# Moving the next pair's projections, turns and Gram matrix to earlier steps of a polynomial-attention loop, and one expert's weight load behind the row scatter

## What is computed

```python
xn = layernorm(x)
# graph convolution: normalised adjacency counts times xn @ W
# attention with a polynomial in place of the exponential, 12 heads of 64:
q, k, v = (qkv[0] * SCALE, qkv[1], qkv[2])
A = einsum('bhnd,bhmd->bhnm', q, k)
numerator = 1.0 + A + 0.5 * A * A
attn = numerator / numerator.sum(axis=-1, keepdims=True)
out = einsum('bhnm,bhmd->bhnd', attn, v)      # then @ w_proj + b_proj
x = x + gnn + attention
# switch feed-forward: 8 experts, at most 195 tokens each, the best first
h = gelu(einsum('ecd,edf->ecf', buf[:E], w1) + b1)
o = einsum('ecf,efd->ecd', h, w2) + b2
x = x + where(keep, o[routes, dest_c], xf) * prob_max
```

## Time and profile before

| | us |
|---|---|
| median of 3 runs | 1183.08 |
| the profiled execution's own time | 1182.01 |
| its span, first to last instruction | 1180.3 |
| the six pairs of heads (steps 0 to end), about | 206.8 to 685.6 |
| one of the first five turns | 79.7 |
| TensorE busy / VectorE busy / ScalarE busy over the span | 932.1 / 723.7 / 458.4 |

### The profile page before, as it was taken

The page is one execution under the profiler, slowest core; times in us unless marked ns, Lnnn a source line. Parts: engine busy times, 40 slices in busy tenths (PEclk is TensorE's granted clock), DMA queues, the critical chain, the costliest instruction groups (busy, mean ns, idle before and its releaser), DMA issues.

```text
span 1180.3 us, 15086 instructions
## 1 busy us (share of the span) xinstructions
PE 932.1 (79%) x5250; PEld 889.0 (75%) x5250; DVE 723.7 (61%) x1357; ACT 458.4 (39%) x678; POOL 307.2 (26%) x204
## 2 busy tenths in 40 slices
PE   1138757899998998999988669889999975199970
PEld 1138756898897997988978559789999974199960
DVE  6249981677778777777777745564444536066633
ACT  1211012666666676666666601111010111156520
POOL 2013345656455553564640000000000002200003
PEclk9569978999999999999999889989999985599995
DMA  8986765233534345326342266463525213769988
GB/s 232 296 287 193 191 165 106 23 58 48 83 60 57 68 65 100 57 22 100 57 66 62 85 105 155 98 172 97 145 77 147 76 60 122 215 188 283 279 199 261
DMA packets 143288, 152.24 MB, mean 129 GB/s; under 512 B 72282, under 2 KB 119869, under 8 KB 142092
## 3 DMA queue, kind: packets, MB, share of 16 engines
q1 hardware_dynamic: 113292, 128.99, 41.5%
q0 software_dynamic: 29952, 22.68, 11.8%
HBM read 97.16 MB, written 46.78 MB: 122 GB/s over the span
## 4 chain that ended last, share of the span: by engine, by line
PE 54%; DVE 16%; DMA 11%; ACT 7%; issue 6%; SPq 2%; POOL 2%; DVEq 0%; POOLq 0%; ACTq 0%
PE ps L1631 12%; PE ps L1633 11%; PE ps L1632 11%; PE ps L1017 7%; DVE eqs L430 5%; DMA kb<-keyd 4%; PE ps L1001 4%; PE ps L1002 4%; ACT Ph L699 2%; ACT Pf L721 2%; DMA rows<-oE 1%; DVE Pl L875 1%; DMA Cs<-counts 1%; POOL rows L1372 1%; PE ps L1265 1%
## 5 line engine op out<-in xcount | busy, mean ns | idle before, releaser
L356 POOL DMA_INDIRECT counts<-countc,idxu x157 | 270.3, 1721 | 303.4 <-DMA counts<-countc,idxu 245.3
L875 DVE SCALAR_TENSOR_TENSOR Pl<-Pf,Ph 125x832 fp32r<-125x832 f32 (+1 forms) x180 | 184.6, 1027 | 111.7 <-ACT Ph L699 105.9
L721 ACT ACTIVATE Pf<-ps 125x832 f32<-125x832 f32 (+1 forms) x180 | 155.5, 864 | 129.2 <-PE ps L1002 119.3
L1017 PE MATMUL ps<-Ph,vsb 125*128 125x416 f32 (+1 forms) x360 | 130.5, 363 | 4.6 <-DVE Pl L875 4.6
L1017 PE MATMUL ps<-Pl,vsb 125*128 125x416 f32 (+1 forms) x360 | 126.9, 352 | 0.0
L1372 POOL DMA_INDIRECT rows<-XF,slots x10 | 14.8, 1480 | 375.7 <-DVE slots L1487 373.0
L1631 PE MATMUL ps<-wH,XH 128*125 128x384 f32 x240 | 86.2, 359 | 21.3 <-DVE VS L469 14.3
L1631 PE MATMUL ps<-XH,wqkH 128*128 128x416 f32 (+1 forms) x216 | 81.4, 377 | 17.4 <-DVE wqkL L766 9.2
L1632 PE MATMUL ps<-wL,XH 128*125 128x384 f32 x240 | 84.6, 352 | 0.0
L1633 PE MATMUL ps<-wH,XL 128*125 128x384 f32 x240 | 84.3, 351 | 0.0
L699 ACT ACTIVATE Ph<-Pf 125x832 fp32r<-125x832 f32 (+1 forms) x90 | 79.9, 895 | 0.7
(11 more groups left out here) (228 smaller groups left out, 2174.8 us busy)
## 6 DMA issues: line engine op xcount, KB each, us to landing
Cs<-counts SPq DMA_DIRECT2D x20, 546.9 KB
kb<-keyd SPq DMA_DIRECT2D x9, 1024.0 KB
w1s<-L_ffn_w SPq DMA_DIRECT2D x8, 1152.0 KB, 8.7
w2s<-L_ffn_w SPq DMA_DIRECT2D x8, 1152.0 KB
odram<-OHL SPq DMA_DIRECT2D x12, 625.0 KB, 7.9
oS<-odram SPq DMA_DIRECT2D x10, 750.0 KB, 4.8
vdram<-VS SPq DMA_DIRECT2D x10, 672.0 KB
vsb<-vdram SPq DMA_DIRECT2D x12, 560.0 KB
```

The costliest lines, as they stand in the source:

```text
L356: pool.indirect_dma_start(out=counts, out_offset=bass.IndirectOffsetOnAxis(ap=idxu[:, c:c + 1], axis=0), in_=countc[:, c:c + 1], in_offset ...
L721: act.activation(Pf[:, i % RING, :, 0:w], ps[0:T, 2 * (i % 2):2 * (i % 2) + 2, 0:w], ACT.Square, bias=1.0).then_inc(sq_done, 1)
L875: dve.scalar_tensor_tensor(out=p, in0=f, scalar=1.0, in1=h.bitcast(F32), op0=ALU.add, op1=ALU.subtract).then_inc(p_lo, 1)
L1017: ins = pe.matmul(ps[:, 4 + s % 2, 0:w], vsb[:, 2 * kp + t, a, :], part[:, m % RING, t, 0:w], start=(kp == 0 and t == 0 and part is Ph), s ...
```

## The change

The steps of the next pair's work in a turn are laid out anew: K projected from steps 5, 9 and 13, turned at 17, 20 and 23, its Gram matrix at 26, and Q's three chunks from steps 19, 25 and 30. Q's third chunk is thus made in the turn before, and for the first pair before the loop. The row sums of the own pair come some four steps earlier. In the experts, SyncE waits for the scatter and loads expert 0's rows before it loads w1 and w2 of expert 1.

```diff
-        QUAD_AT, TOTAL_AT, INVERSE_AT = (3, 5, 8), (11, 12, 13), 16
-        PROJ_AT, TURN_AT, GRAM_AT = (7, 13, 20, 24, 29), (24, 27, 30), 32
+        QUAD_AT, TOTAL_AT, INVERSE_AT = (0, 2, 4), (7, 8, 9), 12
+        PROJ_AT, TURN_AT, GRAM_AT = (5, 9, 13, 19, 25, 30), (17, 20, 23), 26
         SLICES = 3
-        READ_AT = (11, 16, 23, 27, 32)
-        OWN_READ_AT = 3
-        SECOND_AT = (1, 3, 6, 9, 13, 18)
-        FIRST_AT = (24, 25, 26, 28)
-        LATE_AT = (2, 5)
+        READ_AT = (8, 12, 16, 22, 28, 33)
+        SECOND_AT = (1, 3, 4, 6, 8, 10)
+        FIRST_AT = (17, 18, 20, 24, 29)
+        LATE_AT = 2
...
@@ ScalarE, before the loop
-            for g in (3, 4):
+            for g in (3, 4, 5):
                 read_kq(0, g)
             hi_part(0, 0, 3)
+            hi_part(0, 0, 4)
@@ ScalarE, turn
-                    if i == OWN_READ_AT:
-                        read_kq(j, 5)
...
-                    if i in LATE_AT:
-                        hi_part(0, j, 4 + LATE_AT.index(i))
+                    if i == LATE_AT:
+                        hi_part(0, j, 5)
@@ VectorE, before the loop and in the turn
+            lo_part(0, 0, 4)
...
-                    if i in LATE_AT:
-                        lo_part(0, j, 4 + LATE_AT.index(i))
+                    if i == LATE_AT:
+                        lo_part(0, j, 5)
@@ TensorE, before the loop and in the turn
             project(0, 4)
+            project(0, 5)
...
-                    if i < SLICES:
-                        project(j, 5, i * KT // SLICES, (i + 1) * KT // SLICES)
                     if not last and i >= PROJ_AT[0]:
-                        g = max(g for g in range(5) if PROJ_AT[g] <= i)
+                        g = max(g for g in range(6) if PROJ_AT[g] <= i)
@@ SyncE, experts
+            sp.wait_ge(sent, 16 * NT)
+            load_rows(0, 0)
             sp.wait_ge(we_lo, 1)
             load_w1(1)
+            load_rows(1, 1)
             sp.wait_ge(we_lo, 2)
             load_w2(1)
-            sp.wait_ge(sent, 16 * NT)
-            load_rows(0, 0)
-            load_rows(1, 1)
```

## The result

The changed kernel takes **1188.45 us** (median of 5 runs, 1187.34 to 1189.24), the kernel before 1182.15 on the same chip (1181.35 to 1184.69). The ratio is 1.0048, 95% interval 1.0034 to 1.0063: slower, where 1177.0 was forecast. The profiled execution took 1187.86 us; its span is 1186.0.

The account below looks back on a forecast made before the run. TensorE's matmuls and gaps bound the first five turns, something else the last, where ScalarE stalls for weights. 4.5 + 2.5 - 7.9 - 5.0 = -5.9 us gave 1177.0 us, range 1165 to 1187.

Parts of the forecast that it names:

- Parts 1 and 2: Five full turns: old gaps go, minus 7.4 us each; new gaps come, plus 7.9; plus 2.5 in all.
- The four old gaps: Full turn, TensorE's waits at steps 5, 7, 30 and 32, 1.50 to 1.77 us each: all go.
- the last rival: Full turns, step 23: TensorE's clock falls in the 2.35 us gap, plus 12.5 us, 1189.5; chance 0.04.
- Part 3: Before the loop: three projection slices and ScalarE's read now in series, plus 4.5 us.
- Part 4: Last turn: earlier inverse lets the next weights load sooner, stall shrinks from 7.38 to 0.6 us; minus 7.9 in all.
- a lo part fewer and an earlier Pl(1): Last turn: one low part fewer on VectorE (0.58 us) and an earlier low part of P (0.5), minus 1.1.
- Part 5: Start of the experts: scattered rows land 5.5 us sooner, 0.5 given back for w1; minus 5.0 us.
- The price of w1's late landing: Experts: expert 1's w1 lands some 9 us later, which may delay ScalarE; cost 0 to 1 us, taken as 0.5.
- The other rivals: Gaps halved (chance 0.20), VectorE late (0.15), last turn's stall kept, 1184 (0.06), scatter no sooner, 1182 (0.05).
- Gaps half as long: Full turns: shorter queues make the new gaps 5.9 us instead of 7.9; 10 us lower, 1167; chance 0.20.
- VectorE late at the start: Start of each turn: VectorE late, 2.5 us more per turn, plus 12.5, 1189.5; chance 0.15.
- The signs to look for: Profile after: full turn 80.2 us; over 81, or a window at clock 0.5, would mean one of the slow rivals.

Follow-up runs that it names:

- e4: The changed kernel with ten additional matmuls, results unused, on TensorE in the gap at step 23: 1182.17 us, ratio 1.0002 to the kernel before.
- e7: The changed kernel with VectorE's sum over K taken after the split of K's third turned group: 1177.03 us, ratio 0.9956 to the kernel before.
- e1: The changed kernel with SyncE's order of the experts' first loads put back; the pairs keep the new schedule: 1187.37 us, ratio 1.0045 to the kernel before.
- e5: The kernel before with only the own pair's last quadratics, sums and inverse drawn forward: 1190.83 us, ratio 1.0078 to the kernel before.
- e3: The changed kernel with K's third group of transposes moved from step 23 to 25, Gram matrix from 26 to 28: 1182.69 us, ratio 1.0009.
- e12: e8 with the inverse's transposition at step 15 and not at 12: 1177.35 us, ratio 0.9969 to the kernel before.
- e2: The kernel before with the new SyncE order of the experts' first loads alone: 1180.26 us, ratio 0.9978 to the kernel before.
- e10: e8 with K's third group of transposes at step 24 and the Gram matrix at 27, one step later each: 1173.26 us, ratio 0.9927.
- e8: The changed kernel with the split of the next pair's third K chunk asked for at step 21, not 20: 1176.70 us, ratio 0.9956.
- e11: The changed kernel with five additional matmuls, results unused, on TensorE in the gap at step 23: 1180.35 us, ratio 0.9998 to the kernel before.

## Why the prediction was wrong, point by point

- **What bounds the turns** (TensorE's work and its gaps in the first five, the stall in the last): right.
- **Parts 1 and 2.** The four old gaps went. The new ones came where they were put: step 23 at 2.40 (forecast 2.35), step 20 at 0.58 (0.8), step 13 at 0.28 (0.55), steps 30 and 31 at 0.93 and 0.91 (0.9 and 0.8), the start and step 5 at 1.73 and 0.69 (2.25 together). The weight loads stand idle for 8.91 us of the third turn where it was 8.45 (the forecast's 7.9 and 7.4 leave out the shortest): +0.5, as forecast. Without a fall of the clock a turn takes 80.1 to 80.2, the forecast's 80.2.
- **The step that failed is the last rival**, "TensorE's clock falls in the new gap of 2.35 us", which I gave 0.04 and nothing in the sum. It came in every full turn. It was priced at 5 us of half clock, 2.5 us a turn; it lasted from about 435.6 to 439 and cost 1.6. That is 8.0 in all by the profiles, the largest part of a miss of some 11. The changed kernel without its falls is e4: 1.0002. The reason given against it was one idle time of 2.0 us at a clock of 1.00, taken as the rule for 2.35. The window of the earlier trace rows ends 0.8 us behind that gap, too early to tell, since the third turn's fall begins 0.9 us behind its gap; in the trace the clock stays at 1.00 until 649, so the reading was right and the step from it was not. One stretch shows neither a bound nor a chance: 2.03 us let it fall in none of five turns (e7), 2.40 in four of five (e1) and in five of five (the changed kernel), and e5's shorter ones, close together, in four; and in e3 2.95 and 2.97 us let it stand in two turns. The section of the Trainium skill cited there ("TensorE: Matmul & The Clock Gate", "HAM oscillation") says that idle gaps slow the clock and the burst behind them; the trace agrees in kind, with 2.40 us of idle time and 0.50 behind it. The waits in that section's example in the Trainium skill are of 3 to 5 us; here a shorter one was enough. I had argued it away.
- **Part 3**, before the loop: +4.2 against +4.5. The first scores came at 212.5, and 1.2 of that had already passed before anything that was changed.
- **Part 4**, the last turn: -7.4 against -7.9, and the wait for the weights is gone; e12 brings wait and length back. The sum is better than its terms: the stall went whole (7.38 us, counted as 6.8), and ScalarE comes to the split 40.3 us into the turn, as it would have before without its wait (40.4). Of the 1.1 us for a lo part fewer and an earlier Pl(1) nothing is seen; the fall of the clock 30 us into this turn may hide it.
- **Part 5**, the experts: -5.0 was too much. The profile shows 1.7 us, the hunk alone 2.6. In part 5 the scatter's data was to move at 215 to 260 GB/s from 3.3 us behind the first issue, and to be through 3.4 us behind the last one. In the profile after it moves from 5 us behind the first issue (1003.03) until about 1027, 7.6 us behind the last (1019.42): 3.8 MB in 19 us, 200 GB/s. It touches 254 only for a while, as the windows below show; it begins and ends slowly. The 189 GB/s of the earlier trace rows were nearer than the 215 to 260 of the forecast. The price of w1's late landing, 0.5, stays open: ScalarE's wait of 1.60 us in e2 is seen, a cost to TensorE isn't.

```profile
1008.00:1010.00 2.00, 0.00 (x0) 0.00 (x0) 0.08 (x1) 0.00 (x0) 1.70 (x2) 0.50 0.28 74
...
1018.00:1020.00 2.00, 0.00 (x0) 0.00 (x0) 0.00 (x0) 0.00 (x0) 1.70 (x2) 0.50 0.93 254
...
1026.00:1028.00 2.00, 0.00 (x0) 0.00 (x0) 0.00 (x0) 0.00 (x0) 0.00 (x0) 0.50 0.31 111
```

- **The other rivals.** Gaps half as long: no, the two gaps behind short queues, at 13 and 20, were each about a quarter of a us shorter than counted, the rest as counted. VectorE late at the start: it was, 1.73 us in one gap, but this replaced gaps already counted and stayed under the 1.2 us a turn from which it decides. With later transposes it grows, to 2.97 us in e3 and 2.37 in e10. The signs to look for named a turn over 81 with a window at 0.5 in it, and that is what the profile shows.

## What to carry to other kernels

In a loop whose TensorE is nearly full, a new schedule is to be judged by where it gathers its idle time, not only by how much it has in all: 8.45 us in pieces below 1.8 cost nothing more, 8.91 with one piece of 2.40 cost 1.6 us a turn more. The longest piece is not the whole rule: three of at most 1.6 us, close together, did the same in e5, and 2.97 did nothing in two turns of e3. Read the granted clock in windows of 2 us behind the longest gap, and take other engines' work out from ahead of the wait (e8, e10) before moving the wait itself. Where that can't be done, a few matmuls whose results nobody uses win the clock back (e4, e11).

## What was not expected of the hardware

- The same gap of 2.40 us in the same code let the clock fall in one turn and not in the next; what else decides was not found. Nor does the fall start at a fixed distance: 0.4 us behind the gap in the changed kernel's first turn, 1.4 in its fifth, at once in e1's fourth. A fall cost 1.6 us at step 23, where TensorE sets the pace, and 0.9 at a turn's start (e3, e10), where it waits for others anyway.
- Five additional matmuls, about 1 us of work in an idle stretch of 2.4, kept the clock at 1.00 in five turns of five.
- In the last turn of e5 the clock stayed at 0.50 for 10.2 us, although TensorE was busy throughout (634.80 to 645.00).
